# A fused tower's cosine attention: norm products by a row limit and a row scale, the residual term on ScalarE

## The reference, cut to what matters

```python
h = tok(x, W, b)                                  # [16, 374, 256]
y = layernorm(h)
norms = norm(y, axis=-1)
dots = einsum('bil,bjl->bij', y, y)
sim = dots / maximum(norms[:, :, None] * norms[:, None, :], 1e-8)
h = h + einsum('bij,bjl->bil', softmax(sim), y) + y
h = h + experts(layernorm(h))                     # router, q, k, v by expert, causal attention, o by expert
```

## Time and profile before

| | us |
|---|---|
| median of 3 runs | 810.95 |
| the runs | 809.52, 810.95, 2638.78 |
| span of the profiled execution, first to last instruction | 807.9 |

### The profile page before, as it was taken

How to read it: one execution, slowest core, us unless ns; L and a number is a source line. 1 busy time by engine, 2 the same in 40 slices (tenths; PEclk the granted TensorE clock), 3 DMA queues, 4 the chain that set the end, 5 groups by cost and what they waited for, 6 DMA issues and landing times.

```text
span 807.9 us, 17941 instructions
## 1 busy us (share of the span) xinstructions
PE 739.3 (92%) x5338; PEld 456.8 (57%) x5338; DVE 573.2 (71%) x1469; ACT 339.7 (42%) x752; POOL 500.6 (62%) x634
## 2 busy tenths in 40 slices
PE   4797897999999999999999898999999899999995
PEld 3565664656565656556565556565565556565652
DVE  4375577878787868686877778686878687767635
ACT  2475442434343444243353434342534434343343
POOL 5244327467575859586776758594857767684334
PEclk9899999999999999999999999999999999999998
DMA  5643102020202010010101010100101020101000
GB/s 153 166 153 73 59 1 50 1 57 14 57 13 56 12 49 17 12 52 6 55 12 56 12 56 12 49 19 10 52 8 53 12 56 12 56 14 47 14 14 25
DMA packets 30637, 33.27 MB, mean 41 GB/s; under 512 B 4624, under 2 KB 26512, under 8 KB 30608
## 3 DMA queue, kind: packets, MB, share of 16 engines
q1 hardware_dynamic: 22800, 28.64, 12.1%
q10 hardware_dynamic: 7808, 4.27, 2.0%
HBM read 26.65 MB, written 6.25 MB: 41 GB/s over the span
## 4 chain that ended last, share of the span: by engine, by line
PE 32%; POOL 30%; issue 14%; DVE 12%; DMA 5%; ACT 4%; POOLq 2%; DVEq 1%; ACTq 0%; SPq 0%
PE bank L1343 24%; POOL region_a L546 9%; POOL region_c L524 5%; POOL region_c L527 3%; POOL region_b L536 3%; POOL region_b L538 3%; DVE region_b L929 3%; PE bank L1289 3%; POOL xhl L492 2%; POOL small L472 2%; PE bank L1325 2%; ACT region_c L733 2%; DVE stats L911 2%; DMA xm<-in_L_ffn_v_proj_dram 1%; ACT xhl L647 1%
## 5 line engine op out<-in xcount | busy, mean ns | idle before, releaser
L1343 PE MATMUL bank<-xm,w_qkv 128*128 128x374 f16 x2304 | 415.0, 322 | 3.4 <-DVE xm L1022 3.3
L1343 PEld LDWEIGHTS bank<-xm,w_qkv 128*128 128x128 f16 x2304 | 221.5, 98 | 147.1 <-DVE xm L1022 3.7
L1343 PE MATMUL bank<-w_o,aoT 128*128 128x512 f16 x576 | 155.7, 383 | 3.7 <-DVE aoT L934 1.5
L1022 DVE TENSOR_TENSOR xm<-xT,mask_all 128x1496 f16<-128x1496 f16 x128 | 150.6, 1190 | 8.0 <-DMA mask_all<-d_mask 7.7
L945 DVE SCALAR_TENSOR_TENSOR h<-bank,out_w,h 128x256 f32 (+1 forms) x192 | 91.9, 479 | 74.9 <-ACT region_c L733 74.6
L733 ACT ACTIVATE region_c<-bank,out_w 128x256 f32<-128x256 f32 x192 | 88.7, 469 | 128.6 <-PE bank L1343 128.5
L546 POOL TENSOR_SCALAR region_a<-rnorm_row,small 128x384 f32<-128x384 f32 (+2 forms) x48 | 86.1, 1795 | 27.4 <-DMA rnorm_row<-d_rnorm 22.8
L524 POOL TENSOR_TENSOR region_c<-region_c 128x512 f32<-128x512 f32 x47 | 64.7, 1376 | 30.6 <-ACT region_c L733 24.9
L1343 PEld LDWEIGHTS bank<-w_o,aoT 128*128 128x128 f16 x576 | 50.1, 98 | 55.6 <-DVE h L945 14.3
L929 DVE TENSOR_SCALAR region_b<-h,moments,small 128x256 f32 (+1 forms) x96 | 33.8, 408 | 31.5 <-POOL small L474 29.7
L530 POOL TENSOR_TENSOR h<-region_c,h 128x256 f32 (+1 forms) x47 | 41.9, 892 | 16.0 <-POOL region_c L527 11.4
(11 more groups left out here) (160 smaller groups left out, 1070.6 us busy)
## 6 DMA issues: line engine op xcount, KB each, us to landing
mask_all<-d_mask SPq DMA_DIRECT2D x32, 384.0 KB, 3.9
region_c<-in_x_dram SPq DMA_DIRECT2D x16, 256.0 KB
out_dram<-h SPq DMA_DIRECT2D x32, 128.0 KB
rnorm_row<-d_rnorm SPq DMA_DIRECT2D x16, 192.0 KB, 3.5
region_c<-in_x_dram SPq DMA_DIRECT2D x16, 118.0 KB
out_dram<-h SPq DMA_DIRECT2D x16, 118.0 KB
xm<-in_L_ffn_q_proj_dram ACTq DMA_DIRECT2D x2, 512.0 KB, 6.5
xm<-in_L_ffn_k_proj_dram ACTq DMA_DIRECT2D x2, 512.0 KB, 5.6
```

The lines of the kernel that those rows point to most:

```text
L1022: v.tensor_tensor(xm[:, e, :, 0:T], xT[1][:, :, :, 0:T].rearrange("p a c t -> p (a c) t"), mask_all[:, e, 0:T].unsqueeze(1).broadcast_to([ ...
L1343: last = t_.matmul(dst, left[lp], right[rp], start=(starts and k == 0), stop=(stops and k == 2), skip_group_check=True)
```

## The change

The table goes. The product of norms under a limit is taken apart: `min(r_i * r_j, 1/eps) = r_i * min(r_j, 1/(eps * r_i))`. VectorE multiplies the dots by `min(r_j, limit_i)` in one scalar_tensor_tensor (`rnorm_row` from SBUF, the dots from PSUM), and r_i goes into the scale of the exponential. The limit and the scale are columns of `small[0]`, made by `row_scales`, six small GpSimd ops after norm_rows(0). It also makes the scale and bias with which ScalarE computes the residual term straight from h: `hx = h * (1 + rstd) - mean * rstd`. The norms are stored in DRAM in token order.

```diff
@@ norms_out
-                sp.dma_start(d_rnorm[g, :].rearrange("(p t) -> p t", p=P), small[0][:, 5, :]).then_inc(s_rn_stored, 16)
+                with nc.allow_non_contiguous_dma(reason="one norm a token, stored in the order of the tokens"):
+                    sp.dma_start(d_rnorm[g, :].rearrange("(t p) -> p t", p=P), small[0][:, 5, :]).then_inc(s_rn_stored, 16)
@@ norms_in
-                    sp.wait_ge(s_invn_ready, NT * g).then_inc(s_sp_passed, 1)
+                    sp.wait_ge(s_cos_ready, NT * g).then_inc(s_sp_passed, 1)
@@ norm_rows
-                    pool.wait_ge(s_invn_ready, NT * b).then_inc(s_pool_passed, 1)
+            def row_scales(b):
+                sm, mean = small[0], moments[0][:, :, 0]
+                if later(b):
+                    pool.wait_ge(s_hx_ready, NT * b).then_inc(s_pool_passed, 1)
+                g.tensor_scalar(sm[:, 8, :], sm[:, 1, :], 1.0, None, ALU.add).then_inc(s_res_scale1, 1)
+                g.tensor_tensor(sm[:, 3, :], mean, sm[:, 1, :], ALU.mult).then_inc(s_pool1b, 1)
+                pool.wait_ge(s_pool1b, 2 * b + 1).then_inc(s_pool_passed, 1)
+                g.tensor_scalar(sm[:, 9, :], sm[:, 3, :], -1.0, None, ALU.mult).then_inc(s_res_bias1, 1)
...
+                if later(b):
+                    pool.wait_ge(s_cos_ready, NT * b).then_inc(s_pool_passed, 1)
+                    pool.wait_ge(s_exp1_hi, NT * b).then_inc(s_pool_passed, 1)
+                g.tensor_tensor(sm[:, 3, :], sm[:, 2, :], sm[:, 5, :], ALU.mult).then_inc(s_pool1b, 1)
+                g.tensor_scalar(sm[:, 6, :], sm[:, 5, :], 1.0 / (LN_SCALE * LN_SCALE), None,
+                                ALU.mult).then_inc(s_exp_scale1, 1)
+                pool.wait_ge(s_pool1b, 2 * b + 2).then_inc(s_pool_passed, 1)
+                g.tensor_scalar(sm[:, 7, :], sm[:, 3, :], 1.0 / COS_EPS, None, ALU.mult).then_inc(s_limit1, 1)
@@ step of GpSimd
-                if f is not None and not early(m):
-                    rest_of_residual(f)
...
                     norm_rows(0, g1, 1.0, 1e-38)
+                    row_scales(g1)
...
-                    spread_norms(g1)
@@ before the loop, GpSimd
             norm_rows(0, 0, 1.0, 1e-38)
+            row_scales(0)
             low_1(0)
-            spread_norms(0)
-            rest_of_residual(0)
             norm_rows(0, 1, 1.0, 1e-38)
-            spread_norms(1)
+            row_scales(1)
             norm_rows(1, 0, LN_SCALE ** 4, NORM_EPS * NORM_EPS)
             low_1(1)
-            rest_of_residual(1)
@@ ScalarE, exp_cosines (twice)
-                                 scale=1.0 / (LN_SCALE * LN_SCALE))
+                                 scale=small[0][:, 6, t:t + 1])
@@ ScalarE, new; ahead of exp_cosines(f) in a step and for head 0, behind it for head 1
+            def rest_of_residual(f):
+                act.wait_ge(s_res_scale1, f + 1)
+                act.wait_ge(s_res_bias1, f + 1)
+                if later(f):
+                    act.wait_ge(s_h2_ready, NT * f)
+                for t in range(NT):
+                    a.activation(hx[:, t, :], h[:, f, t, :], ACT.Identity, bias=small[0][:, 9, t:t + 1],
+                                 scale=small[0][:, 8, t:t + 1]).then_inc(s_hx_ready, 1)
@@ VectorE, norm_apply
-                if n == 0 and later(b):
-                    dve.wait_ge(s_hx_ready, b).then_inc(s_dve_passed, 1)
@@ VectorE, cosines
-                dve.wait_ge(s_invn_ready, NT * f + t + 1)
+                if t == 0:
+                    dve.wait_ge(s_rn_loaded, 16 * (f + 1))
+                    dve.wait_ge(s_limit1, f + 1)
...
-                v.tensor_tensor(cosine[:, t, t * P:T], work[t % 2][:, t * P:T], inv_norms[:, t, t * P:T],
-                                ALU.mult).then_inc(s_cos_ready, 1)
+                v.scalar_tensor_tensor(cosine[:, t, t * P:T], rnorm_row[:, t * P:T], small[0][:, 7, t:t + 1],
+                                       work[t % 2][:, t * P:T], ALU.min, ALU.mult).then_inc(s_cos_ready, 1)
```

More of the change, by code:

```diff
@@ L82, in audio_tower_kernel @@
         moments = [sb(f"moments{n}", [P, NT, 2]) for n in (1, 2)]
-        small = [sb(f"small{n}", [P, 6, NT]) for n in (1, 2)]
+        small = [sb(f"small{n}", [P, 10 - 4 * n, NT]) for n in (0, 1)]
         xs = [part(region_b, n * NT * C, NT, C) for n in (0, 1)]
@@ L89, in audio_tower_kernel @@
         rnorm_row = sb("rnorm_row", [P, TP])
-        inv_norms = part(region_a, 0, NT, TP)
         cosine = part(region_a, NT * TP, NT, T)
@@ L94, in audio_tower_kernel @@
         inv_sum1 = sb("inv_sum1", [P, NT])
-        hx_scaled = part(region_b, 2 * NT * C, NT, C)
         hx = part(region_b, 3 * NT * C, NT, C)
@@ L199, in audio_tower_kernel @@
         s_rnorm1 = sem("rnorm1")
+        s_exp_scale1 = sem("exp_scale1")
+        s_limit1 = sem("limit1")
+        s_res_scale1 = sem("res_scale1")
+        s_res_bias1 = sem("res_bias1")
+        s_pool1b = sem("pool1b")
         s_xs1 = sem("xs1")
@@ L217, in audio_tower_kernel @@
         s_att_done = sem("att_done")
-        s_hx_s = sem("hx_s")
         s_hx_ready = sem("hx_ready")
@@ L530, in add_tile @@
                 g.tensor_tensor(h[:, n, t, :], prod_sum[:, 2, :], h[:, n, t, :], ALU.add).then_inc(s_tile_ready, 1)
[L532 to L546, removed]
-                                    rnorm_row[:, :].rearrange("p (b a) -> p a b", a=NT)[:, t:NT, :], small[0][:, 5, t:t + 1],
-                                    1.0 / COS_EPS, ALU.mult, ALU.min).then_inc(s_invn_ready, 1)
             def low_probs(n):
@@ L574, in step @@
                     add_tile(n, 0)
-                if g1 is not None:
-                    if not early(m):
-                        low_1(g1)
-                    spread_norms(g1)
+                if g1 is not None and not early(m):
+                    low_1(g1)
                 if n is not None:
@@ L674, in exp_cosines @@
                         act.wait_ge(s_att_done, NT * f)
+                    if t == 0:
+                        act.wait_ge(s_exp_scale1, f + 1)
                     a.activation(exp1[:, t, t * P:T], cosine[:, t, t * P:T], ACT.Exp, bias=log_p[:, :],
-                                 scale=1.0 / (LN_SCALE * LN_SCALE))
+                                 scale=small[0][:, 6, t:t + 1])
                     a.activation(exp1_hl[:, 0, t, t * P:T], cosine[:, t, t * P:T], ACT.Exp, bias=log_p[:, :],
-                                 scale=1.0 / (LN_SCALE * LN_SCALE)).then_inc(s_exp1_hi, 1)
+                                 scale=small[0][:, 6, t:t + 1]).then_inc(s_exp1_hi, 1)
+            def rest_of_residual(f):
[6 more added lines that the diff above has]
+                                 scale=small[0][:, 8, t:t + 1]).then_inc(s_hx_ready, 1)
             def turned_rows_2(f):
@@ L741, in step @@
                     if not early(m):
+                        rest_of_residual(f)
                         exp_cosines(f)
@@ L811, in _ @@
             a.activation(gate_tmp[:, 1, :], gate_tmp[:, 0, :], ACT.Exp, scale=-1.0).then_inc(s_gate_exp, 1)
+            rest_of_residual(0)
             exp_cosines(0)
@@ L825, in _ @@
             exp_cosines(1)
+            rest_of_residual(1)
             route_exp(0)
@@ L1049, in residual @@
             def residual(f):
-                dve.wait_ge(s_hx_ready, f + 1).then_inc(s_dve_passed, 1)
+                dve.wait_ge(s_hx_ready, NT * (f + 1)).then_inc(s_dve_passed, 1)
                 for t in range(NT):
```

4 lines of the change are left out of this document (3 added, 1 removed).

## The result

The changed kernel took **905.07 us** (median of 4 runs, 903.03 to 905.86) against 810.24 for the kernel before: ratio **1.1175**, 95% interval 1.1151 to 1.1198. The forecast was 812, in a range of 797 to 829. The profiled execution spans 903.1 us, 95.2 more than before.

The account below looks back on a forecast made before the run. TensorE, busy 92% of the span, was taken as the bound, so only its waits could be won. Terms -3.5 + 3 + 0.6 + 1.3 = +1.4 on 807.9 gave 809.3; 3.1 to the median made 812, range 797 to 829.

Parts of the forecast that it names:

- Step 6: Norms stored in token order: 4-byte pieces lengthen the store's landing by 0.5 us, 0.1 reaching a step, +1.3 us in all.
- rival A: The norms' round trip through DRAM becomes the bound: landing +1.5 us, about 1.5 to 2 a step, 835 us; chance 0.16.
- Step 1: Table gone from GpSimd: its adds move among VectorE's mask products, so the cosines begin 1.0 to 1.9 us later.
- How the two engines meet: VectorE mask products and GpSimd two-tile adds or subtracts exclude each other; the table does not hold VectorE up (0.92 us).
- Step 2: Residual to ScalarE: 1.3 us hidden in idle time, VectorE's residual some 0.7 us sooner, TensorE's 4.7 us wait at L1470 gone.
- Step 3: Table and residual together in the loop: step 44.28 us against 44.05, +0.23 a step, +3 us over 13 steps.
- rival B: The relief of GpSimd wins and its adds fit between pair sums: steps of 43.4 us, 800 us; chance 0.22.
- Step 4: Cosines as scalar_tensor_tensor (540 ns against 535) and the exponential's scale from a column: nothing, -0.1 to +0.1 us each.
- Step 5: row_scales, six small GpSimd ops: 2.5 us hidden in GpSimd's idle time to within 0.3, +0.05 us a step.
- Step 7: Before the loop: without the table norm_rows starts earlier, so TensorE's work at 81.8 us comes at 78.3, -3.5 us.
- rival D: The start gives nothing: another stall before the loop replaces the one before 81.79, 816 us; chance 0.10.

Follow-up runs that it names:

- e5: Kernel before plus twelve timed stores at its end: adjacent 4-byte pieces 8.63 to 9.37 us, 384 pieces 128 bytes apart 1.73 us.
- e1: Changed kernel with the norms stored as 12-byte pieces again and VectorE reading the row with a stride: 802.11 us, ratio 0.9933.
- e3: Changed kernel, 4-byte store kept, with SyncE serving the mask's round trip ahead of loading the norms: 847.87 us, ratio 1.0517.
- e13: e6 with GpSimd's adds of tile 1 held back until behind the sixth mask product of the step: 786.14 us, ratio 0.9695.
- the square: Step lengths of four kernels with 12-byte stores, residual on GpSimd or ScalarE: with table 43.99 or 42.66 us, without 45.72 or 43.66.
- e6: e1 with the mask's round trip ahead of loading the norms, and head 0's residual behind its exponentials on ScalarE: 790.86 us, ratio 0.9755.

## Why the prediction was wrong

*Step 6, the norms in token order, is the step that failed.* I took +0.5 us on the landing. SyncE's wait for it grew from 2.14 to 8.07 us, +5.9. I had the right chain (the mask's store queued behind the wait, mask 0 late) and a step "at the edge". The size came from the mean packet of SyncE's queue, 0.069 us, scaled by count. But count is the one thing that e5 shows not to matter: 128 pieces cost what 384 cost. Nor is it the packets' time that grew: for most of the wait no packet moves. The 12-byte pieces of the kernel before lie side by side too, and show little of it (2.1 to 2.5 us, 1.47 when 128 bytes apart).

*The bound was right and was not used.* The same step said "at most three times the landing, +6". That end stood in the text and not in the range: rival A was priced at +1.5 us only. With its own slack of 0.7 us, +5.9 gives 5.2 a step, 68 over 13 steps; the idle time that e1 took away is 69.5. The mechanism of rival A, the mask's store queued behind the wait, is what happened, and e3, which takes the queueing away, gets back 57 of the 103 us. The other 46 stay, since the slow store delays the mask's store also from another queue; neither the forecast nor rival A had that. Nor did they have that the mask's own store takes 4.15 instead of 2.48 us in the change, so the nearness of 68 to 69.5 is in part luck.

*Rival A also left out the clock.* After a stall of 5.7 us TensorE ran at a mean granted clock of 0.73; 30.9 us of the 100.4 between the changed kernel and e1 are the same matmuls taking longer.

*Step 1, the adds among the masks: right in kind, too large in effect.* The ledger had the masks end 1.0 to 1.9 us later. In e1 the mean mask product is 1277 ns against 1190 before, 0.7 us over eight, and e13 prices the adds among them at 0.48 a step. In the changed kernel the mean is only 1114: there the masks wait for DMA, and in the step shown tile 0's adds and two of tile 1's three are over when they begin.

*How the two engines meet: half the reading.* That the table does not hold VectorE up stands. But the masks hold the table up, which the prediction's own rows say: 4.0 us before the loop, where no mask runs, and 5.40 in the step (up to 6.17 in others). So at L546, where the prediction found no exclusion, one engine does hold up the other, with GpSimd as the one that pays.

*Step 2, the residual on ScalarE: hidden, as said, and worth more than said.* L1470's wait and L1055's for GpSimd are gone, and no wait in the loop shows the ScalarE time. It is 591 ns an activation, 1.6 us a head, and not under 0.5 and 1.3. And I counted 0.7 us of head start; the square gives 1.3 with the table and 2.1 without. Alone it makes the kernel 2.9% faster.

*Step 3, together.* +0.23 a step was forecast; with the store taken out, e1 has -0.32. That is between rival B's -0.6 and the forecast, by errors of both signs, so its nearness is no merit of the sum.

*Step 4, the column scale, was called nothing.* 92 ns lies inside the ±0.1 that I gave for each, but six a step were not summed: 0.35 us a step reach the end, some 4.5 us in 13. The new cosine instruction of 374 columns is 594 ns, not 540.

*Step 5, row_scales: right.* 2.45 us (472.70 to 475.15), and the router's next op followed after 0.18 us of idle time.

*Step 7, before the loop: half.* The stall of 4.74 us at 81.79 is gone. But the residual's activations ahead of head 0's exponentials make TensorE wait 2.4 to 2.6 us there, in place of 0.7, and the 27 matmuls behind it took 4.79 us instead of 3.14, at a granted clock of 0.65. The start of e1 is 0.6 us later than before, not 3.5 earlier: rival D's outcome. e6, with the residual behind the exponentials and the mask first, starts 7.0 earlier than before.

## What to carry to other kernels

When a change alters the layout of a small store, look at how close its pieces lie in DRAM and at what is queued or in flight behind it; if the nearest row is of another form, carry the upper bound through to the time. Before taking work from an engine, ask whom it kept apart: the table was cheap and held GpSimd's adds away from VectorE's mask products. Price one instruction's extra operand by the number of times that it stands on the path.

## What was not expected of the hardware

- Stores of 4-byte pieces to adjacent DRAM addresses take 7.1 to 9.4 us, whether 128, 256 or 384 pieces; at a spacing of 16 bytes or more 1.5 to 2.1, and 12-byte pieces side by side 2.1 to 2.5.
- For most of that time no DMA packet moves: the DMA share is 0.00 for 6.3 of 8.4 us.
- Such a store, in flight, stretches a 6 KB store behind it from 1.5 us (e6) to 5.1 and more (e3), and from another engine's queue to 4.5 and more (e7); the second store lands when a slow one by itself would.
- The granted clock of TensorE fell to a mean of 0.73 behind a stall of 5.7 us, and to 0.65 behind one of 2.4, where 27 matmuls took 1.65 us longer.
